# In the last body of a cross-attention and MoE kernel, scores and maxima of a head group come in two pairs, the first one group ahead

## The reference, cut to what matters

```
q = rms_norm(linear(x, q_w, q_b), norm_q_w).reshape(B, L, NH, HD)
k = rms_norm(linear(ctx_txt, k_w, k_b), norm_k_w).reshape(B, -1, NH, HD)
k_img = rms_norm(linear(ctx_img, k_img_w, k_img_b), norm_k_img_w).reshape(B, -1, NH, HD)
scores = jnp.einsum('bqhd,bkhd->bhqk', q, k) * scale      # in attention(), once for text, once for image
probs = jax.nn.softmax(scores, axis=-1)
...
out = (txt_x + img_x).reshape(B, L, DIM)
return linear(out, o_w, o_b)
...
x = x + xattn(layernorm(x), ctx_2048)
x = x + ffn(layernorm(x))     # gate, softmax, top 2 of 8 experts, gelu, gelu, weighted sum
```

## Time and profile before

| | us |
|---|---|
| median of 3 runs | 837.37 (837.31 to 839.81) |
| the profiled execution, its own time | 834.9 |
| its span in the trace | 832.7 |
| PE busy | 770.6 (93%) |
| DVE busy | 599.6 (72%) |
| ACT busy | 490.9 (59%) |
| POOL busy | 240.4 (29%) |
| body 7, first score matmul to the last exponential | 344.26 to 376.79 |
| first work of the expert loop on PE | 404.16 |

### The profile page before, as it was taken

One profiled execution on the slowest core, in us unless ns is written; L12 is line 12 of the kernel. 1 busy time (PEld: TensorE's weight loads), 2 busy tenths in 40 slices (PEclk: granted clock), 3 DMA queues, 4 the chain that ended last, 5 costly groups with the idle time before them and its releaser, 6 DMA issues.

```text
span 832.7 us, 17460 instructions
## 1 busy us (share of the span) xinstructions
PE 770.6 (93%) x5995; PEld 666.4 (80%) x5995; DVE 599.6 (72%) x1269; ACT 490.9 (59%) x1136; POOL 240.4 (29%) x302
## 2 busy tenths in 40 slices
PE   4889898999999989787899999999999999999994
PEld 3667676767676767555798999999999999999993
DVE  6767878787978787776676757676676758676664
ACT  4377777767676777786245555554545555554543
POOL 3523334342434333223300505032140505032010
PEclk9989999999999999999999999999999999999998
DMA  9820102011020201142756665748566665648561
GB/s 308 291 83 4 56 6 58 38 35 61 24 72 13 83 13 35 31 175 89 260 203 223 233 232 208 248 172 285 191 248 220 238 233 210 250 172 286 194 220 64
DMA packets 29205, 126.28 MB, mean 152 GB/s; under 512 B 4204, under 2 KB 4220, under 8 KB 19424
## 3 DMA queue, kind: packets, MB, share of 16 engines
q1 hardware_dynamic: 23696, 109.80, 37.6%
q0 software_dynamic: 5456, 15.81, 5.3%
HBM read 108.42 MB, written 18.74 MB: 153 GB/s over the span
## 4 chain that ended last, share of the span: by engine, by line
PE 71%; DVE 11%; ACT 10%; issue 4%; DMA 1%; POOL 0%; SPq 0%; ACTq 0%; DVEq 0%; POOLq 0%
PE tiles L1176 6%; PE tiles L1178 6%; PE tiles L1177 6%; PE scores L1478 4%; PE scores L1480 4%; PE scores L1479 4%; PE ptb L1291 4%; PE pvb L1178 3%; PE pvb L1177 3%; PE ptb L1177 3%; PE pvb L1176 3%; PE ptb L1176 3%; PE ptb L1178 3%; PE scores L1281 2%; ACT scr L658 2%
## 5 line engine op out<-in xcount | busy, mean ns | idle before, releaser
L920 DVE TENSOR_TENSOR w<-scr,w 128x2048 fp32r<-128x2048 f32 x75 | 170.8, 2288 | 59.5 <-ACT w L684 59.5
L684 ACT ACTIVATE w<-scr 128x2048 fp32r<-128x2048 f32 x76 | 144.8, 1909 | 54.8 <-PE scores L1480 54.8
L514 POOL DMA_INDIRECT out_dram<-scr,tok x17 | 18.0, 1058 | 298.7 <-DVE scr L1155 296.2
L666 ACT ACTIVATE scr<-scr,rsum 112x257 f32<-112x257 f32 x128 | 66.7, 521 | 60.6 <-DVE rsum L904 60.6
L1176 PE MATMUL tiles<-w 128*128 128x256 f32 (+1 forms) x288 | 82.9, 288 | 0.6
L1176 PE MATMUL tiles<-c,w 128*128 128x258 f32 (+2 forms) x272 | 79.3, 291 | 2.6 <-DVE c L1129 1.2
L1177 PE MATMUL tiles<-w 128*128 128x256 f32 (+1 forms) x288 | 81.2, 282 | 0.0
L1178 PE MATMUL tiles<-w 128*128 128x256 f32 (+1 forms) x288 | 81.2, 282 | 0.0
L1143 DVE CAST w<-scr 128x256 fp32r<-128x256 f32 (+1 forms) x144 | 41.9, 291 | 52.5 <-ACT scr L774 52.5
L1178 PE MATMUL tiles<-c,w 128*128 128x258 f32 (+2 forms) x272 | 76.9, 283 | 0.0
L1177 PE MATMUL tiles<-c,w 128*128 128x258 f32 (+2 forms) x272 | 76.7, 282 | 0.0
(11 more groups left out here) (223 smaller groups left out, 2332.0 us busy)
## 6 DMA issues: line engine op xcount, KB each, us to landing
scr<-in_dram SPq DMA_DIRECT2D x76, 1024.0 KB, 4.9
scr<-in_dram SPq DMA_DIRECT2D x8, 750.0 KB, 4.6
scr<-slots_d SPq DMA_DIRECT2D x10, 528.0 KB, 5.4
scr<-in_dram SPq DMA_DIRECT2D x10, 512.0 KB, 8.8
slots_d<-rows SPq DMA_DIRECT2D x8, 528.0 KB, 11.1
xn<-in_dram SPq DMA_DIRECT2D x9, 256.0 KB
xb<-in_dram SPq DMA_DIRECT2D x8, 224.0 KB, 2.7
xr<-in_dram SPq DMA_DIRECT2D x8, 224.0 KB, 2.6
```

Source lines behind the costliest of these rows:

```text
L666: act.activation(probs[0:L, s, 0:IMG], probs[0:L, s, 0:IMG], ACT.Copy, scale=rsum[0:L, g, s, 0:1]).then_inc(S["normal_img"], 1)
L684: act.activation(EH[slot], raw[slot], ACT.Copy).then_inc(S["eh_done"], 1)
L920: dve.tensor_tensor(EL[slot], raw[slot], EH[slot].bitcast(F32), ALU.subtract).then_inc(S["el_done"], 1)
```

## The change

Only body 7 is touched.

- PE: the scores of groups 1, 2 and 3 are made in two pairs. The pair of heads 0 and 1 of group g+1 stands at the start of slot 4g+2 (slots 2, 6, 10) and waits for the exponentials of heads 0 and 1 of group g only; it raises a semaphore of its own, `pair_ready`. The pair of heads 2 and 3 stands in slot 4g, where all four stood. Each pair is 6 matmuls. Group 0 stays as it was.
- DVE: the maxima of the first pair move with it to slots 2, 6 and 10, behind `invert_sums` and ahead of `attended`.
- ACT: `weigh` stands at the beginning of slots 4, 8 and 12 too, ahead of `normalise` of the head before; only slot 0 keeps it at the end.
- Key halves: POOL's in slots 0, 3 and 7 (before 1, 5 and 8), DVE's in slots 1, 5 and 8 (before 2, 6 and 10).

```diff
--- before.py
+++ after.py
@@ -66,6 +66,8 @@
 
 KEYS_HIGH_AT = {1: 1, 5: 2, 8: 3}
 KEYS_LOW_AT = {2: 1, 6: 2, 10: 3}
+LAST_HIGH_AT = {0: 1, 3: 2, 7: 3}
+LAST_LOW_AT = {1: 1, 5: 2, 8: 3}
 SQUARES_AT = {1: "k0", 2: "k1", 5: "kx", 9: "k2", 10: "k3"}
 LAG = 2
 FIRST, LAST, DONE = 0, B - 1, B
@@ -247,7 +249,7 @@
...
-            "s_ready", "max_done", "exp_done", "inverted", "normal_img", "normal_txt", "t_ready", "pt_done",
+            "pair_ready", "s_ready", "max_done", "exp_done", "inverted", "normal_img", "normal_txt", "t_ready", "pt_done",
@@ -561,8 +563,9 @@
                 for h in range(NH):
                     if h == 0 and has_prep(b):
                         split_ctx_high(b + 1, 1)
-                    if h in KEYS_HIGH_AT and has_heads(b):
-                        split_keys(b, p, KEYS_HIGH_AT[h])
+                    keys_at = LAST_HIGH_AT if fixed(b, LAST) else KEYS_HIGH_AT
+                    if h in keys_at and has_heads(b):
+                        split_keys(b, p, keys_at[h])
                     if h == 1 and has_prep(b):
                         pool.wait_ge(S["ms_read"], b + 1)
                     if h in SQUARES_AT and has_prep(b):
@@ -713,7 +716,7 @@
                         split_out_weight(OUT_HIGH_AT[h])
                     if h == 10 and has_prep(b):
                         evacuate("k3", b, p)
-                    if h % 4 and has_heads(b):
+                    if (h if fixed(b, LAST) else h % 4) and has_heads(b):
                         weigh(b, p, h)
                     if h == 0 and has_tail(b):
                         normalise(b - 1, NH - 1)
@@ -733,7 +736,7 @@
 
                         act.wait_ge(S["gate_in"], b)
                         act.activation(xt, pvb[:, 0:NC * L].rearrange("p (c q) -> p c q", c=NC), ACT.Copy).then_inc(S["xt_done"], 1)
-                    if h % 4 == 0 and has_heads(b):
+                    if (h == 0 if fixed(b, LAST) else h % 4 == 0) and has_heads(b):
                         weigh(b, p, h)
                     if h == 0 and has_route(b) and not fixed(b, DONE):
                         gate_exp(b - 2)
@@ -892,7 +895,10 @@
 
             def maxima(b, g, i):
 
-                dve.wait_ge(S["s_ready"], NC * b + g + 1)
+                if fixed(b, LAST) and g and i == 0:
+                    dve.wait_ge(S["pair_ready"], g)
+                else:
+                    dve.wait_ge(S["s_ready"], NC * b + g + 1)
                 of = nmax[0:L, g % 2, 2 * i:2 * i + 2, :]
                 dve.tensor_reduce(of[:, :, 0], scores[0:L, 2 * i:2 * i + 2, 0:IMG], AX.X, ALU.max, negate=True)
                 dve.tensor_reduce(of[:, :, 1], scores[0:L, 2 * i:2 * i + 2, IMG:KEYS], AX.X, ALU.max, negate=True).then_inc(S["max_done"], 1)
@@ -1015,13 +1021,17 @@
                     if h and has_heads(b):
                         invert_sums(b, h - 1)
                     if h % 4 == 0 and has_heads(b):
-                        maxima(b, h // 4, 0)
+                        if not (fixed(b, LAST) and h):
+                            maxima(b, h // 4, 0)
                         maxima(b, h // 4, 1)
                     if h == 14 and has_prep(b):
                         split_queries_low(b + 1, 1 - p)
                         split_keys_low(b + 1, 1 - p, 0)
-                    if h in KEYS_LOW_AT and has_heads(b):
-                        split_keys_low(b, p, KEYS_LOW_AT[h])
+                    keys_at = LAST_LOW_AT if fixed(b, LAST) else KEYS_LOW_AT
+                    if h in keys_at and has_heads(b):
+                        split_keys_low(b, p, keys_at[h])
+                    if fixed(b, LAST) and h % 4 == 2 and h < NH - 2:
+                        maxima(b, h // 4 + 1, 0)
                     if h == 10 and has_prep(b):
                         add_squares(b, 0)
                         add_squares(b, 1)
@@ -1281,6 +1291,16 @@
                         mm = pe.matmul(scores[0:L, i, 0:KP], q[of, g, :], k[of, g % 2, :], start=(n == 0), stop=(n == 2))
                 mm.then_inc(S["s_ready"], 1)
 
+            def score_pair(b, p, g, i):
+
+                pe.wait_ge(S["kl_done"], NC * b + g + 1)
+                pe.wait_ge(S["exp_done"], NH * b + 4 * g - 2 + 2 * i)
+                for n, (q, k) in enumerate(((qH, kH), (qH, kL), (qL, kH))):
+                    for s in (2 * i, 2 * i + 1):
+                        of = slice(HD * s, HD * s + HD)
+                        mm = pe.matmul(scores[0:L, s, 0:KP], q[of, g, :], k[of, g % 2, :], start=(n == 0), stop=(n == 2))
+                mm.then_inc(S["s_ready"] if i else S["pair_ready"], 1)
+
             def transpose(b, h):
 
                 pe.wait_ge(S["normal_img"], NH * b + h + 1)
@@ -1332,7 +1352,12 @@
             def body(b, p):
                 for h in range(NH):
                     if h % 4 == 0 and has_heads(b):
-                        score(b, p, h // 4)
+                        if fixed(b, LAST) and h:
+                            score_pair(b, p, h // 4, 1)
+                        else:
+                            score(b, p, h // 4)
+                    if fixed(b, LAST) and h % 4 == 2 and h < NH - 2:
+                        score_pair(b, p, h // 4 + 1, 0)
                     if h < LAG:
                         if has_tail(b):
                             transpose(b - 1, NH - LAG + h)
```

## The result

| | before | changed |
|---|---|---|
| median of 22 runs of each, taken together | 837.9 us | 840.46 us |
| ratio | | 1.0032, 95% interval 1.0019 to 1.0045 |
| profiled execution, its own time (before: the one of the earlier trace rows) | 834.9 | 839.78 |
| its span | 832.7 | 837.6 |
| head 0's first exponential to the first work of the experts | 57.82 | 62.03 |

I had forecast 837.1, with a range of 835.0 to 839.4 and a chance of 0.82 on no difference that can be told. It is 0.3% slower, 1.1 us above the upper end of the range. Of the 4.9 us between the two spans 4.2 lie between head 0 of body 7 and the expert loop. The spans are further apart than the medians (2.6 us), because the profiled execution of the kernel before, at 834.9, lies 3.0 us under its median and that of the changed kernel only 0.7 under its own.

The account below looks back on a forecast made before the run. Bound: one dependent chain from body 7 to the expert loop, with ACT's waits to watch. Leads ran 1.1, 0.4, -0.3, 0.35; the last, less 0.05 for hand-overs, gave 837.37 - 0.3 = 837.1 us, range 835.0 to 839.4.

Parts of the forecast that it names:

- Everything reaches the end one for one: Body 7 to the expert loop is one dependent chain, so what body 7 gains or loses reaches the end in full.
- A pair costs PE 0.70: Each early pair of score matmuls takes PE 0.70 us, the upper bound; the lower was 0.35.
- Slots 0 to 3 cost nothing: Group 1's early pair and maxima fit idle time on PE and DVE, and earlier key halves delay nothing: no cost.
- Slots 4 to 9, lead 1.1, 0.4, then lag 0.3: ACT leads 1.1 us at head 5, 0.4 at head 6; slot 6's pair delays a reciprocal, so lags 0.3 at head 9.
- Slots 10 to 15, 0.65 back: Group 3's early pair is covered, turning the lag of 0.3 us into a lead of 0.35 at head 13.
- The clock: Slot 2's pair adds 0.6 us of PE work before 349.1; the slow stretch may go, bringing `attended` 0.4 us earlier.
- another count of slow stretches: Sign of being wrong: another count or place of slow clock stretches, able alone to move the time by more than the sum.
- Rival C: A slow clock stretch moves over the experts' first work, costing 1.7 us, two 3.4: 839.1 to 840.8; chance 0.12.
- Rival B: DVE's queue becomes the wait in slots 6 and 10, pair maxima holding up reciprocals: 0.9 us slower, 838.3; chance 0.14.
- Rival A: Slot 6's pair hides and all three boundaries pay, 2.15 us plus 0.4 from the clock: 834.8 us; chance 0.19.

Follow-up runs that it names:

- after2: The changed kernel again, unaltered; 839.31 us, ratio 1.0035 to the kernel before.
- a_busy8: The changed kernel with 8 instead of 2 spare matmuls at the end of slot 1 of body 7; 838.14 us, ratio 1.0027 to before.
- split_in_place: The kernel before with scores of groups 1, 2 and 3 made as two pairs back to back in slot 4g; 837.26 us, ratio 1.0024.
- a_fill: The changed kernel with spare matmuls raised to 8, 5, 5, 4 at the end of slots 1, 2, 7, 8; 835.14 us, ratio 0.9988 to before.
- b_fill: The kernel before with spare matmuls raised to 8, 5, 5, 7, 5 ending slots 1, 2, 7, 9, 13; 834.33 us, ratio 0.9974.
- g3_fill: The changed kernel with groups 1 and 2 as before, spare matmuls 8, 5, 5, 5, 4 ending slots 1, 2, 7, 9, 13; 835.62 us, ratio 0.9964.
- b_half: The kernel before, spare matmuls ending slots 2, 3, 8, 9 of body 7 replaced by three passes two row groups wide; 839.94 us, ratio 1.0026.
- b_full3: The kernel before with three instead of two full spare matmuls ending slots 2, 3, 8, 9 of body 7; 838.05 us, ratio 1.0001.
- after3: The changed kernel again, in a later session; 840.59 us, ratio 1.0026 to before.
- a_wide2: The changed kernel with pair passes four row groups wide (three in slot 6) by matmuls nobody reads; 838.64 us, ratio 1.0001 to before.

## Why the prediction was wrong, point by point

- **Everything reaches the end one for one.** Nearly right: after2 is 4.25 us behind before at head 13's exponential (30.72 against 26.47 after head 0) and 4.40 behind at the experts (62.22 against 57.82).
- **A pair costs PE 0.70.** Right to 0.01: in a_busy8 354.94 to 355.64 and 360.07 to 360.77. That two pairs one behind the other would cost no more than one (split_in_place) I had not seen.
- **Slots 0 to 3 cost nothing.** Wrong by 0.7 at 2.4 GHz, hidden in the profile of before by its own slow stretch. At 2.4 GHz the attention product of slot 2 is done earlier, and `attended` then waits behind the moved maxima. In a_fill DVE goes from the maxima to `attended` without idle time, 4.82 us after head 0's exponential (345.99):

```profile
349.90 0.69 DVE L903 TENSOR_REDUCE nmax<-scores 112x2 f32<-112x514 f32 x1
350.50 0.40 DVE L904 TENSOR_REDUCE nmax<-scores 112x2 f32<-112x236 f32 x1
350.81 0.33 DVE L918 TENSOR_SCALAR af<-pvb,vbias 128x112 f32<-128x112 f32 x1
```

In b_fill DVE waits for the product instead, and `attended` comes 4.13 after head 0's exponential (344.24):

```profile
348.37 0.34 DVE L912 TENSOR_SCALAR af<-pvb,vbias 128x112 f32<-128x112 f32 x1 [0.38 <-PE pvb L1314]
```

- **Slots 4 to 9, lead 1.1, 0.4, then lag 0.3.** Right as mechanism and, at 2.4 GHz, in size: counted from the gate's matmul (6.73 us after head 0 in a_busy8, 6.39 in b_fill), the lead is 1.08 at head 5 and 0.45 at head 6, and the lag 0.44 at head 9. From the gate's matmul (353.59 before, 353.92 in a_busy8, so 0.33 more) I had head 5 at 356.49, head 6 at 358.69, head 6's reciprocal at 363.84 (it came at 363.96) and head 9 at 366.27. The trace of a_busy8:

```profile
356.53 0.47 ACT L661 ACTIVATE scr<-scores,nmax 112x257 f32<-112x257 f32 x1
...
358.68 0.47 ACT L661 ACTIVATE scr<-scores,nmax 112x257 f32<-112x257 f32 x1
...
366.39 0.49 ACT L661 ACTIVATE scr<-scores,nmax 112x257 f32<-112x257 f32 x1
```

- **Slots 10 to 15, 0.65 back.** Right in sign and near in size: a_fill makes good 0.7 between heads 9 and 13, g3_fill, where only this part is made, gains 0.42. The sum at one clock is then some 0.5 us slower, not 0.3 faster, and slots 0 to 3 are the term that was missing.
- **The clock.** This is the step that failed. I took the pair in slot 2 for 0.6 us more of PE work, which could only take the slow stretch away, and priced it at 0.4 us of gain. It did the opposite: the stretch grew from 3.4 to 13.7 us over the one part of body 7 where PE's queue is the way, and cost some 3.6 us more in the trace, by the estimate above. The prediction had named another count of slow stretches as a sign of being wrong, but gave it no price in this place.
- **The rivals.** Rival C had a slow stretch, but over the experts' first work; that did not happen. That the measured 840.46 lies in its 839.1 to 840.8 is luck. Rival B, a wait in DVE's queue, came true in slots 0 to 3, where it had not been looked for. Rival A was off: the output projection and the pair in slot 6 left no room.

## What to carry to other kernels

When PE's work is split into narrower pieces, or moved to where it has just been idle, read the granted clock around the place before the waits: here the sum of waits was off by 0.8 us, and the clock, which was left out of it, took some 3.6 in the trace. A term read from a profile at 1.2 GHz may also hide a wait that shows at 2.4. Compare two kernels at the same clock, by traces whose slow stretches agree or by each run's mean clock, before a difference is put down to order. Spare work in front of the part where PE is the way was worth more than the reordering, some 0.25% alone (0.9974 and 0.9976) and 0.36% with the one early pair that paid in the trace.

## What the runs showed of the hardware

- Row groups (32 of the 128 rows of the PE array each) overlap across the passes: six matmuls on groups 0 and 1 followed by six on groups 2 and 3 took 0.71 us to the next instruction (split_in_place), as much as the six alone (0.70, a_busy8).
- Passes on two of four row groups went with 45.8 us at 1.2 GHz a run, against 37.1 with full matmuls about as long at the same places (b_half, b_full3), and lone pairs with 43.2, against 35.7 for the same pairs filled to four groups, in slot 6 to three (after3, a_wide2).
- At 1.2 GHz a lone pair took 1.28 us instead of 0.77, an attention product 1.35 instead of 0.79 (the changed kernel and a_busy8).
